# Earlier weight loads, five gathers at once and the last sums on three engines in a tower of convolution, attention and sorted experts

## Chip, cores and metric

One core of a Trainium2 chip. The time is that of the device in microseconds (us), one execution of the whole program; lower is better. Before the change it is 224.91 us, the median of 3 runs (224.11 to 225.05).

## What is computed

`x` is 8 batches of 375 rows of 128 numbers, all fp32. Three layers follow each other:

```python
# 1: per batch, on x transposed
h = silu(conv1d(xt, w_compress)); h = silu(conv1d(h, w_main, padding=1)); h = conv1d(h, w_expand)
y = layer_norm(h + x) * g + b
ff = gelu(y @ w_ff1.T + b_ff1) @ w_ff2.T + b_ff2
y = layer_norm(ff + y) * g2 + b2
h = max over 3 neighbouring rows of y            # 373 rows a batch
# 2: attention within a batch
n = layernorm(h); q = (n @ Wq + bq) * scale; k = n @ Wk + bk
h = h + softmax(q @ k.T) @ n
# 3: 8 experts, the best 2 for each row
n = layernorm(h); gates = softmax(relu(n @ gw1 + gb1) @ gw2 + gb2)
w, idx = top_k(gates, 2); w = softmax(w)
out = h + sum over the two: w * (gelu(n @ we1[e] + be1[e]) @ we2[e] + be2[e])
```

## The kernel before

Each of the five engines has its program written out as a string of pieces, `name.number`: `PE_ORDER` (TensorE, with the PSUM bank behind the colon), `DVE_ORDER` (VectorE), `ACT_ORDER` (ScalarE), `POOL_ORDER` (GpSimd) and `SP_ORDER` (the issuing queue of SyncE, SP here). Each engine goes through its string in order, and semaphores make a piece wait for its inputs. A piece that stands early in a string is thus issued early, and one that waits holds all that stand behind it. Rows of a batch lie as 125 partitions by 3 (`P`, `NJ`).

- Warm-up and first layer. `w.n` are `WARM[n]` plain 128x128 matmuls of the identity into a bank that is free (line 1000; each is two records in the trace). `a1` to `a7` are the convolutions, norms and transposes of the first layer (lines 1001 to 1084), `ft` and `fn` fold the two attention matrices into one (line 1038), `cb` and `bf` prepare bias columns. `xb` on GpSimd (line 528) adds a bias row to `x`, `p1` to `p4` on GpSimd (line 517) make 1/sqrt for the four norms, `l1` to `l4` apply them, on VectorE or ScalarE.
- Attention: `b1`, `bq`, `sc0` to `sc2`, `pt0` to `pt2`, `at` (lines 1091 to 1126), with `prob` and `prob_t` in SBUF.
- Experts. Batches 0, 6 and 7 (`DENSE`) go through all 8 experts: `D1` (line 1181, two per expert, 373 columns), `dg` (gelu on ScalarE, line 660; it reuses one of three `gd` tiles and so waits for `D2` of two experts before), `D2` (line 1188, 12 records), `da` (line 929, VectorE adds the weighted result to `x_sb`; each waits for the one before). They also fill TensorE's time between other pieces.
- Batches 1 to 5 (`SPARSE`) are sorted by expert. `scat` (line 541, GpSimd) scatters their rows into the DRAM buffer `xs`, a run of up to 2048 rows per expert. Then come 37 blocks of 128 rows (`NB` = 8 first blocks of each expert + 29 whose expert is known at run time alone). `rg.n` (line 422) loads a block's place from the table `tab_x` into a register of SP, `lx.n` (line 436) loads the block's rows into one of 18 `blk_x` tiles, `lw.n` (line 444) copies its expert's weights, 321 KB from `w_all`, into one of `WSLOTS` `blk_w` tiles. `lx.n` waits until `T.n-10` is done, `lw.n` until `yv` of the tile's last user is. Then `T.n` (transpose, line 1197), `xT.n` (copy), `L1.n` (line 1204), `gl.n` (gelu, ScalarE, line 671), `L2.n` (line 1213), `yv.n` (bias, VectorE, line 955, into one of `YBUF` tiles `yblk`), `so.n` (line 547: GpSimd scatters the block to its rows in `ys`).
- The end. `yl.n` (line 453) gathers both results of all rows of a sparse batch into `yg`, which has room for three batches, so `yl.3` and `yl.4` wait for the first sums. `fin.n` (lines 964 and 970) is six operations on VectorE that add them, times their weights in `w_top`, to `x_sb`. `out.n` and `od.n` (line 464) store the sparse and the dense batches, three DMAs each.

## Time and profile before

| | us |
|---|---|
| median of 3 runs | 224.91 |
| profiled execution, its time | 223.55 |
| its span, first to last instruction | 221.8 |
| TensorE busy | 206.9 (93%) |
| VectorE busy | 154.2 (70%) |
| ScalarE busy | 136.9 (62%) |
| GpSimd busy | 112.9 (51%) |

The engines are called PE (matmuls; PEld are its weight loads), DVE (VectorE), ACT (ScalarE), POOL (GpSimd) and SP. A `q` behind the name (SPq) marks the engine's sequencer, which issues DMAs. The page cuts the span into 40 slices of 5.5 us and gives each engine's busy share in tenths (9 stands for 90% or more). The chain is followed back from the last instruction to whatever released it. The granted clock of TensorE is 0.996 of full over the whole span.

### The profile page before, as it was taken

How to read it: one execution, taken by the hardware profiler on the slowest of the kernel's cores; microseconds unless marked ns; L12 is line 12 of the kernel's file. 1: busy time of each engine (PE TensorE's matmuls, PEld its weight loads, DVE VectorE, ACT ScalarE, POOL GpSimd, SP SyncE). 2: the span in 40 equal slices, each digit the busy share in tenths (PEclk: the TensorE clock that was granted, in tenths of full speed). 3: DMA queues.
4: the chain of work that ended last, by engine and by line, in shares of the span. 5: the costliest groups of instructions: out<-in, count | busy, mean ns of one | idle time of the engine just before them, and what ended most of it. 6: DMA issues, size and time to landing. Idle time of an engine off the chain costs nothing.

```text
span 221.8 us, 5472 instructions
## 1 busy us (share of the span) xinstructions
PE 206.9 (93%) x1575; PEld 169.1 (76%) x1575; DVE 154.2 (70%) x688; ACT 136.9 (62%) x302; POOL 112.9 (51%) x168
## 2 busy tenths in 40 slices
PE   6997897899999999999999999999999889899990
PEld 6875656668957986798778876889998778699780
DVE  6169899999898998887788953486435333234895
ACT  2124987998889688867578447646645456444430
POOL 7626676720740055747674776005777676572000
PEclk9999999999999999999999999999999999999998
DMA  5999999950010003111211121377696899822673
GB/s 128 247 269 298 318 405 405 401 197 3 0 35 1 3 0 83 50 35 49 70 47 36 38 69 60 74 235 248 192 311 201 296 295 303 286 90 74 189 221 105
DMA packets 25856, 35.30 MB, mean 159 GB/s; under 512 B 4067, under 2 KB 18566, under 8 KB 25827
## 3 DMA queue, kind: packets, MB, share of 16 engines
q1 hardware_dynamic: 23137, 30.79, 43.7%
q0 software_dynamic: 2240, 4.00, 5.8%
q8 instruction: 13, 0.21, 0.4%
q10 hardware_dynamic: 450, 0.16, 0.4%
q14 instruction: 16, 0.13, 0.2%
HBM read 10.61 MB, written 14.39 MB: 113 GB/s over the span
## 4 chain that ended last, share of the span: by engine, by line
PE 73%; DVE 8%; SPq 6%; ACT 5%; issue 4%; DMA 2%; POOL 1%; DVEq 0%; ACTq 0%
PE PS L1188 11%; PE PS L1181 10%; PE PS L1123 7%; PE PS L1105 7%; PE PS L1213 5%; PE PS L1204 5%; PE PS L1000 5%; PE PS L988 4%; PE PS L1112 4%; SPq L444 3%; PE PS L1100 3%; SPq L436 2%; PE PS L1017 2%; DVE acc L964 2%; DMA blk_x<-xs 2%
## 5 line engine op out<-in xcount | busy, mean ns | idle before, releaser
L547 POOL DMA_INDIRECT ys<-yblk,blk_x x37 | 36.0, 972 | 27.5 <-DVE yblk L955 19.3
L517 POOL TENSOR_TENSOR rstd<-mv,mhalf 125x3 f32<-125x3 f32 x32 | 27.7, 866 | 42.3 <-DVE mv L697 42.0
L541 POOL DMA_INDIRECT xs<-rows_x,pos_x x30 | 29.9, 998 | 13.3 <-issue 8.4
L660 ACT ACTIVATE gd<-PS,bias 128x373 f32<-128x373 f32 x48 | 27.1, 574 | 15.4 <-PE PS L1181 10.7
L1181 PE MATMUL PS<-xt_sb,w_all 128*128 128x373 f32 x96 | 35.7, 482 | 0.0
L1188 PEld LDWEIGHTS PS<-w_all,gd 128*125 128x125 f32 x288 | 33.6, 188 | 2.1
L1188 PE MATMUL PS<-w_all,gd 128*125 128x128 f32 x288 | 34.6, 273 | 0.0
L671 ACT ACTIVATE gb_t<-PS,blk_w 128x128 f32<-128x128 f32 x58 | 18.0, 365 | 14.2 <-issue 7.7
L929 DVE SCALAR_TENSOR_TENSOR x_sb<-PS,comb,x_sb 125x128 f32<-125x128 f32 x72 | 20.7, 342 | 5.8 <-PE PS L1188 4.9
L1181 PEld LDWEIGHTS PS<-xt_sb,w_all 128*128 128x128 f32 x96 | 15.7, 190 | 5.0 <-issue 0.9
L955 DVE TENSOR_TENSOR yblk<-PS,blk_w 128x128 f32<-128x128 f32 x29 | 8.4, 290 | 14.9 <-PE PS L1213 14.5
L1105 PE MATMUL PS<-xn_t,q_t 128*125 128x373 f32 x48 | 18.0, 488 | 0.0
L1123 PE MATMUL PS<-xn,prob_t 125*125 125x129 f32 (+1 forms) x144 | 17.6, 275 | 0.0
L1213 PE MATMUL PS<-blk_w,gb_t 128*128 128x128 f32 x116 | 17.4, 277 | 0.0
L1123 PEld LDWEIGHTS PS<-xn,prob_t 125*125 125x125 f32 (+1 forms) x144 | 16.7, 187 | 0.8 <-issue 0.4
L1204 PE MATMUL PS<-xb_t,blk_w 128*128 128x128 f32 x116 | 17.2, 275 | 0.0
L816 DVE COPY xb_t<-PS 128x128 f32<-128x128 f32 x27 | 7.8, 289 | 13.6 <-PE PS L1197 11.1
L1204 PEld LDWEIGHTS PS<-xb_t,blk_w 128*128 128x128 f32 x116 | 15.6, 191 | 1.8 <-issue 0.3
L1213 PEld LDWEIGHTS PS<-blk_w,gb_t 128*128 128x128 f32 x116 | 15.0, 191 | 0.7 <-issue 0.3
L830 DVE TENSOR_REDUCE nmax<-PS 125x1 f32<-125x373 f32 x24 | 12.8, 543 | 2.9 <-PE PS L1105 2.2
L636 ACT ACTIVATE prob_t<-PS 124x373 f32<-124x373 f32 (+1 forms) x23 | 9.9, 482 | 6.2 <-PE PS L1112 5.9
L630 ACT ACTIVATE prob<-PS,nmax 125x373 f32<-125x373 f32 x24 | 12.5, 574 | 1.4 <-DVE nmax L830 1.2
(201 smaller groups left out, 414.1 us busy)
## 6 DMA issues: line engine op xcount, KB each, us to landing
blk_w<-w_all SPq DMA_DIRECT2D x29, 321.0 KB, 3.0
xs<-blank SPq DMA_DIRECT2D x1, 8256.0 KB, 25.8
blk_x<-xs SPq DMA_DIRECT2D x37, 64.5 KB, 3.2
yg<-ys SPq DMA_DIRECT2D x5, 336.0 KB
xt_sb<-in_xt SPq DMA_DIRECT2D x4, 375.0 KB, 5.9
x_sb<-in_x SPq DMA_DIRECT2D x4, 336.0 KB
out<-x_sb SPq DMA_DIRECT2D x8, 168.0 KB
w_all<-in_we SPq DMA_DIRECT2D x1, 1024.0 KB
```

What stands on the lines that cost most here:

```text
L517: pool.tensor_tensor(rstd[i][:, n % 2, :], mv[i][:, n % 2, :, 1], mhalf[:], ALU.pow)\
L541: pool.indirect_dma_start(xs, bass.IndirectOffsetOnAxis(ap=pos_x[:, b // 2, s, i:i + 1], axis=0), rows_x[:, k, s, j, :], None, bounds_chec ...
L547: pool.indirect_dma_start(ys, bass.IndirectOffsetOnAxis(ap=blk_x[n % SLOTS][:, t, D:XW].bitcast(u32), axis=0), yblk[n % YBUF][:, t, :], No ...
L660: act.activation(gd[:, k % GD, c, 0:TP], of("D1", n)[:, 0:TP], ACT.Gelu, bias=bias128[:, 2 + k % E * HC + c:3 + k % E * HC + c]).then_inc( ...
L671: last = act.activation(gb_t[n % 2][:, c, :], of("L1", n)[:, c * BLK:(c + 1) * BLK], ACT.Gelu, bias=w[:, 2 * H + c:2 * H + c + 1])
L929: last = dve.scalar_tensor_tensor(flat(h2[:, b, :])[j], flat(of("D2", n)[0:P, :])[j], w[:, j, b % 2, e:e + 1], flat(h2[:, b, :])[j], ALU.m ...
L1105: pe.matmul(f[0:P, 0:TP], q_t[:, s, OFF[j]:OFF[j] + P], xn_t[:, s, :], start=True, stop=True)\
L1123: last = pe.matmul(f[0:P, j * (D + 1):(j + 1) * (D + 1)], prob_t[0:ROWS[c], s, c, OFF[j]:OFF[j] + P], xn3[0:ROWS[c], s, c, :], start=(c == ...
L1181: pe.matmul(f[:, 0:TP], w_all[:, k % E, c * 128:(c + 1) * 128], x32[:, DENSE[k // E], 0:TP], start=True, stop=True).then_inc(S["D1"], 1)
L1188: last = pe.matmul(f[0:P, j * D:(j + 1) * D], gd[:, n % GD, c, OFF[j]:OFF[j] + P], w_all[:, n % E, H + c * D:H + (c + 1) * D], start=(c == ...
L1204: last = pe.matmul(f[:, c * BLK:(c + 1) * BLK], w[:, c * 128:(c + 1) * 128], xb_t[n % 2][:], start=True, stop=True)
L1213: last = pe.matmul(f[:, t * D:(t + 1) * D], gb_t[n % 2][:, c, t * 128:(t + 1) * 128], w[:, H + c * D:H + (c + 1) * D], start=(c == 0), sto ...
```

## The change

- `WSLOTS` goes from 7 to 14 and `YBUF` from 6 to 12. The seven added weight tiles lie in a tile `late`, which `prob` and `prob_t` use before; `lw.15`, the first that goes there, waits for the last `at`. Eight of the `blk_x` tiles now lie in `blank`. The semaphores of the added tiles are reused ones.
- The gathers `yl` of the five sparse batches go into tiles of their own (two of them in `late`) and no longer wait for a sum.
- `fin.1` and `fin.3` leave VectorE: `fm.1` and `fm.3` on ScalarE multiply the gathered tile in place by the weights (six activations each), and GpSimd adds the two products with two `tensor_tensor` of 125x384.
- New orders on all engines, in which some copies change between VectorE and ScalarE, and `WARM` goes from (12, 15, 5, 3) to (22, 13, 4, 3, 1).

```diff
--- before.py
+++ after.py
@@ -52,9 +52,11 @@
 XW = D + 1
 SLOTS = 18
 LOADS = 10
-WSLOTS = 7
-YBUF = 6
+WSLOTS = 14
+OWN = 7
+YBUF = 12
 YG = 3
+assert NS <= YG + 3
 
 PER = ROWS_X // 128
 RI = max(k for k in range(1, 9) if PER % k == 0)
@@ the orders, their parts that the steps below follow
 PE_ORDER = """
-w.0:0 a1.0:5 w.1:0 ft.0:7 a2.0:6 a2.1:3 w.2:0 a3.0:1 a3.1:4 a1.1:3 cb.0:2 w.3:0 a2.2:7 a2.3:6 fn.0:0 a1.2:1 bf.0:4
+w.0:1 a1.0:0 w.1:2 a2.0:1 a2.1:4 ft.0:5 w.2:0 a3.0:2 a3.1:6 a1.1:5 cb.0:3 w.3:0 a2.2:5 a2.3:7 w.4:1 bf.0:0 fn.0:3
...
-g2.3:0 D1.21:1 D1.22:2 D1.23:0 D1.24:3 D1.25:1 D2.9:7 D2.10:6 D2.11:0 ct.1:2 ct.2:3 bd.1:1 T.0:5 D2.12:2 L1.0:5
+g2.3:6 D1.21:0 D1.22:7 D1.23:3 D1.24:1 D2.9:6 D1.25:4 D2.10:0 D2.11:2 T.0:3 ct.1:1 ct.2:7 L1.0:3 T.1:4 bd.1:1 L1.1:4
...
-L2.31:5 L1.32:1 T.34:2 D1.36:3 L1.33:0 L2.32:5 T.35:1 L1.34:2 L2.33:7 L1.35:6 T.36:0 L2.34:5 D1.37:1 L1.36:4 L2.35:6
-D1.38:2 L2.36:7 D2.15:0 D2.16:5 D1.39:3 D1.40:7 D2.17:1 D2.18:6 D2.19:7 D1.41:1 D1.42:6 D1.43:5 D1.44:2 D2.20:7
-D1.45:4 D1.46:3 D2.21:5 D1.47:1 D2.22:2 D2.23:0
+L1.30:4 T.32:3 L2.29:0 L1.31:2 D1.34:4 L2.30:3 T.33:2 L1.32:0 L2.31:3
+T.34:5 L1.33:6 L2.32:4 T.35:3 L1.34:5 L2.33:0 T.36:1 L1.35:3 L2.34:7 L1.36:4 D1.35:1 L2.35:7 D1.36:6 L2.36:5 D1.37:1
+D2.15:7 D1.38:4 D1.39:2 D2.16:6 D2.17:1 D2.18:0 D1.40:5 D1.41:6 D1.42:2 D1.43:5 D1.44:3 D2.19:7 D2.20:6 D1.45:5
+D2.21:0 D1.46:2 D1.47:7 D2.22:5 D2.23:2
 DVE_ORDER = """
-ft.0 a3.0 a3.1 l1.0 fn.0 cb.0 l1.1 bf.0 a3.2 a3.3 l1.2
+ft.0 a3.0 a3.1 cb.0 l1.0 bf.0 l1.1 a3.2 a3.3 l1.2 fn.0
...
-da.15 da.16 da.17 da.18 da.19 fin.0 fin.1 fin.2 da.20 da.21 fin.3 da.22 da.23 fin.4
+da.15 da.16 da.17 fin.0 da.18 da.19 da.20 fin.2 da.21 fin.4 da.22 da.23
 ACT_ORDER = """
...
-gl.34 gl.35 gl.36 dg.36 dg.37 dg.38 dg.39 dg.40 dg.41 dg.42 dg.43 dg.44 dg.45 dg.46 dg.47
+gl.36 dg.35 dg.36 dg.37 dg.38 dg.39 dg.40 dg.41 dg.42 dg.43 fm.1 fm.3 dg.44 dg.45 dg.46 dg.47
 POOL_ORDER = """
...
-so.27 so.28 so.29 so.30 so.31 so.32 so.33 so.34 so.35 so.36
+so.27 so.28 so.29 so.30 so.31 so.32 so.33 so.34 so.35 so.36 fin.1 fin.3
 SP_ORDER = """
-c4.1 c4.2 c4.3 c4.4 c4.5 rg.8 rg.9 rg.10 rg.11 rg.12 rg.13 rg.14 rg.15 od.0 rg.16 rg.17 rg.18 rg.19 rg.20 rg.21
-rg.22 rg.23 rg.24 rg.25 rg.26 lx.0 lx.1 lx.2 lx.3 lx.4 lx.5 lx.6 lx.7 lx.8 lw.8 lx.9 lw.9 lx.10 lw.10 lx.11 lw.11
...
-lx.27 lw.27 lx.28 lw.28 rg.35 lx.29 lw.29 lx.30 lw.30 lx.31 lw.31 lx.32 lw.32 lx.33 lw.33 lx.34 lw.34 rg.36 lx.35
-lw.35 lx.36 lw.36 yl.0 yl.1 yl.2 od.1 yl.3 out.0 yl.4 out.1 out.2 out.3 od.2 out.4
+c4.1 c4.2 c4.3 c4.4 rg.8 rg.9 rg.10 rg.11 rg.12 lw.8 rg.13 c4.5 lw.9 rg.14 lw.10 rg.15 lw.11 rg.16 lw.12 rg.17 lw.13
+rg.18 rg.19 rg.20 lw.14 lx.0 lx.1 lx.2 lw.15 lx.3 lw.16 lx.4 lx.5 lx.6 lx.7 od.0 lw.17 lx.8 lx.9 rg.21 lx.10 rg.22
...
+lx.22 lx.23 lx.24 lx.25 lx.26 lw.21 lw.22 lw.23 lx.27 rg.28 lw.24 lw.25 rg.29 lx.28 lx.29 rg.30 lw.26 lx.30 lw.27
+lw.28 rg.31 rg.32 lw.29 rg.33 lw.30 lx.31 lw.31 lx.32 lw.32 rg.34 rg.35 lx.33 lw.33 lw.34 lx.34 rg.36 lx.35 lx.36
+lw.35 lw.36 od.1 yl.0 yl.1 yl.2 yl.3 yl.4 out.0 out.1 out.2 out.3 out.4 od.2
@@ -146,7 +148,7 @@
 
 
 
-WARM = (12, 15, 5, 3)
+WARM = (22, 13, 4, 3, 1)
 
 
 ON_ACT = set(pieces(ACT_ORDER))
@@ -237,9 +239,10 @@
         xn_t = sb("xn_t", [D, 2, TP])
         q_t = sb("q_t", [D, 2, TE])
         nmax = sb("nmax", [P, 2, NJ])
-        prob = sb("prob", [P, 2, NJ, TP])
+        late = sb("late", [128, (WSLOTS - OWN) * WROW])
+        prob = late[0:P, 0:2 * NJ * TP].rearrange("p (s j t) -> p s j t", s=2, j=NJ)
         rinv = sb("rinv", [P, NJ])
-        prob_t = sb("prob_t", [P, 2, NJ, TE])
+        prob_t = late[0:P, 2 * NJ * TP:2 * NJ * (TP + TE)].rearrange("p (s j t) -> p s j t", s=2, j=NJ)
         h2 = x_sb
         xn4 = sb("xn4", [P, len(DENSE), NJ, D])
         rows_x = sb("rows_x", [128, NS, 2, NJ, XW])
@@ -276,16 +279,19 @@
         tab_e = sb("tab_e", [1, NDYN], i32)
         tab_x = sb("tab_x", [1, NDYN], i32)
 
-        blk_x = [sb(f"blk_x{i}", [128, NT, XW]) for i in range(SLOTS)]
-        blk_w = [sb(f"blk_w{i}", [128, WROW]) for i in range(WSLOTS)]
+        blank = sb("blank", [128, RI, XW])
+        blk_x = [sb(f"blk_x{i}", [128, NT, XW])[:] for i in range(SLOTS - RI)] + [blank[:, r:r + 1, :] for r in range(RI)]
+        blk_w = [sb(f"blk_w{i}", [128, WROW])[:] for i in range(OWN)]\
+            + [late[:, i * WROW:(i + 1) * WROW] for i in range(WSLOTS - OWN)]
         xb_t = [sb(f"xb_t{i}", [D, BLK]) for i in range(2)]
         gb_t = [sb(f"gb_t{i}", [128, HC, BLK]) for i in range(2)]
         yblk = [sb(f"yblk{i}", [128, NT, D]) for i in range(YBUF)]
-        yg = sb("yg", [P, YG, 2, NJ * D])
+        yg_own = sb("yg", [P, YG, 2, NJ * D])
+        yg = [yg_own[:, i, :, :] for i in range(YG)]\
+            + [late[0:P, i * 2 * NJ * D:(i + 1) * 2 * NJ * D].rearrange("p (s d) -> p s d", s=2) for i in range(NS - YG)]
         acc = sb("acc", [P, NJ, D])
 
         tiny = sb("tiny", [1, 1])
-        blank = sb("blank", [128, RI, XW])
 
         gd = sb("gd", [128, GD, HC, TE])
         comb = sb("comb", [P, len(DPAIRS), NI, E])
@@ -324,11 +330,15 @@
         s_blank = sem("s_blank_out")
         s_copy = [sem(f"s_copy{i}") for i in range(2)]
         s_scat = sem("s_scat")
-        s_yl = [sem(f"s_yl{i}") for i in range(YG)]
+        s_yl = [(sem(f"s_yl{i}"), 0) for i in range(YG)]
         s_out = sem("s_out")
         s_bx = [sem(f"s_bx{i}") for i in range(LOADS)]
-        s_bw = [sem(f"s_bw{i}") for i in range(WSLOTS)]
         s_so = [sem(f"s_so{i}") for i in range(YBUF)]
+
+
+        s_yl += [(S["wt"], 16 * 9), (S["rows"], 16), (s_blank, 16)]
+        s_bw = ([(s, 32) for s in s_x] + [(s, 16) for s in s_xt] + [
+            (S[v], 16 * m) for v, m in (("wc", 1), ("we", 2), ("b64", 2), ("wm", 2), ("rows6", 1), ("wmid", 3))])[:WSLOTS]
 
         def wait(eng, name, value):
             if value > 0:
@@ -361,8 +384,9 @@
             if n < E:
                 eng.wait_ge(S["be1"], 1)
                 return w_all[:, n, :]
-            eng.wait_ge(s_bw[(n - E) % WSLOTS], 16 * ((n - E) // WSLOTS + 1))
-            return blk_w[(n - E) % WSLOTS][:]
+            s, first = s_bw[(n - E) % WSLOTS]
+            eng.wait_ge(s, first + 16 * ((n - E) // WSLOTS + 1))
+            return blk_w[(n - E) % WSLOTS]
 
         def xn4_of(n):
 
@@ -433,29 +457,29 @@
                         sp.wait_ge(s_scat, 16 * NI * NS)
                     wait(sp, "T", n - LOADS + 1)
                     wait_so(sp, n - SLOTS)
-                    sp.dma_start(blk_x[i][:], xs[bass.ds(row_of_block[n], BLK), :].rearrange("(p t) d -> p t d", t=NT))\
+                    sp.dma_start(blk_x[i], xs[bass.ds(row_of_block[n], BLK), :].rearrange("(p t) d -> p t d", t=NT))\
                         .then_inc(s_bx[n % LOADS], 16)
                 if name == "lw":
                     k = n - E
                     if k == 0:
                         sp.wait_ge(S["be1"], 1)
+                    if k == OWN:
+                        wait(sp, "at", B)
                     if k >= WSLOTS:
                         wait(sp, "yv", n + 1 - WSLOTS)
-                    sp.dma_start(blk_w[k % WSLOTS][:], w_all[:, bass.ds(row_of_block[n] // CAP, 1), :].rearrange("p o d -> p (o d)"))\
-                        .then_inc(s_bw[k % WSLOTS], 16)
+                    sp.dma_start(blk_w[k % WSLOTS], w_all[:, bass.ds(row_of_block[n] // CAP, 1), :].rearrange("p o d -> p (o d)"))\
+                        .then_inc(s_bw[k % WSLOTS][0], 16)
                 if name == "yl":
                     if n == 0:
                         for m in range(NB - YBUF, NB):
                             wait_so(sp, m)
-                    if n >= YG:
-                        wait(sp, "ob", n - YG + 1)
                     for lo, hi in SPLIT:
-                        sp.dma_start(yg[lo:hi, n % YG, :, :],
+                        sp.dma_start(yg[n][lo:hi, :, :],
                                      ys[2 * T * n:2 * T * (n + 1), :]
-                                     .rearrange("(s p j) d -> p s (j d)", s=2, j=NJ)[lo:hi]).then_inc(s_yl[n % YG], 16)
+                                     .rearrange("(s p j) d -> p s (j d)", s=2, j=NJ)[lo:hi]).then_inc(s_yl[n][0], 16)
                 if name in ("out", "od"):
                     if name == "out":
-                        wait(sp, "ob", n + 1)
+                        wait(sp, *summed(n))
                         b = SPARSE[n]
                     else:
                         wait(sp, "da", E * (n + 1))
@@ -541,6 +565,13 @@
                     pool.indirect_dma_start(xs, bass.IndirectOffsetOnAxis(ap=pos_x[:, b // 2, s, i:i + 1], axis=0),
                                             rows_x[:, k, s, j, :], None, bounds_check=ROWS_X - 1, oob_is_err=False)\
                         .then_inc(s_scat, 16)
+                if name == "fin":
+
+                    k, b = RANK_POOL["fin", n], SPARSE[n]
+                    wait(pool, "fm", RANK_ACT["fm", n])
+                    pool.tensor_tensor(h2[:, b, :], h2[:, b, :], yg[n][:, 0, :], ALU.add).then_inc(S["obp"], 1)
+                    wait(pool, "obp", 2 * k - 1)
+                    pool.tensor_tensor(h2[:, b, :], h2[:, b, :], yg[n][:, 1, :], ALU.add).then_inc(S["obp"], 1)
                 if name == "so":
                     wait(pool, "yv", n + 1)
                     for t in range(NT):
@@ -609,6 +640,15 @@
                     wait(act, "ht", n // 2 - 1)
                     act.activation(y2_t[:, n // 2 % 2, n % 2, :], of("a7", n)[:, 0:T], ACT.Identity, bias=cols[:, 5:6],
                                    scale=cols[:, 4:5]).then_inc(S[nth("y2", n)[0]], 1)
+                if name == "fm":
+
+                    gathered(act, n)
+                    w = shares(n)
+                    for s in range(2):
+                        for j in range(NJ):
+                            last = act.activation(flat(yg[n][:, s, :])[j], flat(yg[n][:, s, :])[j], ACT.Copy,
+                                                  scale=w[:, s, j, :])
+                    last.then_inc(S["fm"], 1)
                 if name == "hv":
                     wait(act, "hr", n + 1)
                     wait(act, "h2", NJ * (n - 1))
@@ -956,19 +996,17 @@
                                       w.unsqueeze(1).broadcast_to([128, NT, D]), ALU.add)\
                         .then_inc(S["yv"], 1)
                 if name == "fin":
-                    dve.wait_ge(s_yl[n % YG], 32 * (n // YG + 1))
-                    wait(dve, "ob", n)
-                    b = SPARSE[n]
-                    w = w_top[:, b // 2, :, :].rearrange("p s (j b) -> p s j b", b=2)
+                    gathered(dve, n)
+                    k, b, w = RANK_DVE["fin", n] - 1, SPARSE[n], shares(n)
+                    wait(dve, "ob", k)
                     for j in range(NJ):
-                        last = dve.scalar_tensor_tensor(acc[:, j, :], flat(yg[:, n % YG, 0, :])[j], w[:, 0, j, b % 2:b % 2 + 1],
-                                                        flat(h2[:, b, :])[j], ALU.mult, ALU.add)
-                        last.then_inc(S["acc"], 1)
+                        dve.scalar_tensor_tensor(acc[:, j, :], flat(yg[n][:, 0, :])[j], w[:, 0, j, :],
+                                                 flat(h2[:, b, :])[j], ALU.mult, ALU.add).then_inc(S["acc"], 1)
                     for j in range(NJ):
                         if j != 1:
-                            wait(dve, "acc", NJ * n + (2, 2, 3)[j])
-                        last = dve.scalar_tensor_tensor(flat(h2[:, b, :])[j], flat(yg[:, n % YG, 1, :])[j],
-                                                        w[:, 1, j, b % 2:b % 2 + 1], acc[:, j, :], ALU.mult, ALU.add)
+                            wait(dve, "acc", NJ * k + (2, 2, 3)[j])
+                        last = dve.scalar_tensor_tensor(flat(h2[:, b, :])[j], flat(yg[n][:, 1, :])[j], w[:, 1, j, :],
+                                                        acc[:, j, :], ALU.mult, ALU.add)
                     last.then_inc(S["ob"], 1)
 
         @block.tensor
```

## Rows read from the trace of the kernel before

**Rows 1.** Page, part 1 and 2: busy time, then tenths in 40 slices of 5.5 us.

```profile
PE 206.9 (93%) x1575; PEld 169.1 (76%) x1575; DVE 154.2 (70%) x688; ACT 136.9 (62%) x302; POOL 112.9 (51%) x168
...
PE   6997897899999999999999999999999889899990
```

**Rows 2.** Timeline of the start: start us, us, engine, line, operation, tiles, count.

```profile
2.04 4.28 PE L1000 MATMUL PS<-ident 128*128 128x128 f32 x24 [2.04 <-DVE comb_t L711]
...
7.03 3.62 PE L1000 MATMUL PS<-ident 128*128 128x128 f32 x30
...
7.21 0.57 ACT L576 ACTIVATE hc<-PS,bias 128x375 f32<-128x375 f32 x1 [2.39 <-PE PS L1006]
...
10.48 0.27 PE L1038 MATMUL PS<-ident,wk_sb 128*128 128x128 f32 x1
...
10.79 1.21 PE L1017 MATMUL PS<-hc,wm_d 64*64 64x192 f32 x24
```

**Rows 3.** Landing of the loads of xt_sb and of wm_d (answers by tile).

```profile
DMA to landing us min/median/max: 3.3/5.9/6.7
...
DMA to landing us min/median/max: 3.7/4.6/5.4
```

**Rows 4.** Waits of TensorE and of SP: us in total, times, longest.

```profile
PE PS L1197 <- DMA blk_x<-xs: 2.6, 3, 1.0
...
SPq L444 <- DVE yblk L955: 1.4, 1, 1.4
```

**Rows 5.** Chain that ended last, sparse stage and end: start us, us, what.

```profile
186.66 4.08 DMA blk_x<-xs
...
192.02 0.45 PE PS L1204 x4
...
192.57 0.63 PE PS L1181 x2
...
198.72 2.63 PE PS L1188 x24
```

**Rows 6.** Timeline of SP's queue: start us, us of issue, line, tiles.

```profile
139.29 5.35 SPq L436 DMA_DIRECT2D blk_x<-xs  x9
...
173.61 0.49 SPq L444 DMA_DIRECT2D blk_w<-w_all  x1
...
175.80 0.50 SPq L444 DMA_DIRECT2D blk_w<-w_all  x1
...
186.66 0.38 SPq L436 DMA_DIRECT2D blk_x<-xs  x1
...
187.98 0.77 SPq L436 DMA_DIRECT2D blk_x<-xs  x1
```

**Rows 7.** Timeline of the end.

```profile
202.53 2.56 SPq L453 DMA_DIRECT2D yg<-ys  x6
...
207.37 0.87 DVE L964 SCALAR_TENSOR_TENSOR acc<-yg,w_top,x_sb 125x128 f32<-125x128 f32 x3
...
213.40 2.79 PE L1188 MATMUL PS<-w_all,gd 128*125 128x128 f32 x24
...
218.39 0.87 DVE L970 SCALAR_TENSOR_TENSOR x_sb<-yg,w_top,acc 125x128 f32<-125x128 f32 x3
```

**Rows 8.** Timeline around 18 us and 27 us.

```profile
17.99 2.90 POOL L528 TENSOR_TENSOR x_sb<-x_sb,row_be 125x384 f32<-125x384 f32 x3
...
18.06 2.91 DVE L703 TENSOR_SCALAR n<-r,mv,rstd 125x128 f32<-125x128 f32 x3
...
27.40 1.25 ACT L565 ACTIVATE n<-r,nmr,rstd 125x128 f32<-125x128 f32 x3
```

**Rows 9.** Answers by source line, 422 (registers) and 436 (gathers).

```profile
L422 SPq TENSOR_LOAD <-tab_x x29: 261/273/665, 122.4 to 189.5; - x29
...
DMA to landing us min/median/max: 2.2/3.2/3.9
```

**Rows 10.** Timeline, the transpose of the last block (T.36).

```profile
195.41 0.27 PE L1197 MATMUL PS<-ident,blk_x 128*128 128x128 f32 x1
```

More of the change, by code:

```diff
@@ new lines @@
+a2.7:5 a7.0:6 a5.1:7 a3.6:1 a3.7:0 a4.4:6 a7.1:2 a6.2:7 a6.3:5 a4.5:3 hr.0:4 a5.2:1 hr.1:6 a6.4:1 a7.2:7 a4.6:6
+b1.0:2 a7.3:5 b1.1:3 bq.0:2 a6.5:7 sc0.0:4 sc1.0:6 bq.1:2 sc2.0:3 a7.4:5 sc0.1:1 sc1.1:2 a4.7:6 pt0.0:3 pt1.0:0
+pt2.0:4 sc2.1:6 a5.3:4 at.0:0 pt0.1:1 pt1.1:3 pt2.1:5 hr.2:2 a6.6:6 at.1:4 hr.3:5 a7.5:2 h1.0:1 a6.7:3 D1.0:0 b1.2:7
+D1.1:5 D1.2:1 h1.1:6 bq.2:7 a7.6:5 g1.0:0 b1.3:6 sc0.2:2 sc1.2:7 bq.3:1 g2.0:6 a7.7:4 sc2.2:0 sc0.3:1 sc1.3:5 hr.4:2
+pt0.2:3 pt1.2:0 D2.0:7 pt2.2:0 sc2.3:1 hr.5:3 at.2:4 pt0.3:0 pt1.3:6 pt2.3:1 rk.0:5 D1.3:0 at.3:1 ct.0:2 D2.1:5
@@ L163, in ranks @@
     return rank
[L166 removed]
+RANK_ACT, RANK_DVE, RANK_POOL = ranks(ACT_ORDER), ranks(DVE_ORDER), ranks(POOL_ORDER)
 BANK = {tuple(word.split(":")[0].split(".")): int(word.split(":")[1]) for word in PE_ORDER.split()}
@@ L345, in wait_nth, with summed, gathered, shares @@
                 wait(eng, *nth(name, n))
+        def summed(n):
+            return ("obp", 2 * RANK_POOL["fin", n]) if ("fin", n) in RANK_POOL else ("ob", RANK_DVE["fin", n])
+        def gathered(eng, n):
+            s, loads = s_yl[n]
+            eng.wait_ge(s, loads + 32)
+        def shares(n):
+            return w_top[:, SPARSE[n] // 2, :, :].rearrange("p s (j b) -> p s j b", b=2)[:, :, :, SPARSE[n] % 2:SPARSE[n] % 2 + 1]
         def normed_by(i, n):
```

83 lines of the change are left out of this document (38 added, 45 removed).

## The prediction

> **What bounds the kernel now.** I read the page first [rows 1]: TensorE is busy 93% of the span and 9 tenths or more of nearly every slice between 42 and 200 us. The time is therefore TensorE's work plus the stretches in which it starves or does filler, plus what follows its last matmul. The change leaves the matmuls as they are (only warm-up ones are added), so I looked for these stretches in three places.
>
> The start: its timeline [rows 2] shows w.0 (24 records, two per matmul) until 6.3 us, the first convolution a1.0 at once behind it, w.1 (30 records in 3.62 us, 0.12 each) until about 10.4, then a2.0 at 10.79. The landing views [rows 3] say that this wasn't needed: the first load of `xt_sb` was issued at 1.28 and landed 3.3 us later, at 4.6; the second of `wm_d`, issued at 2.65, took 5.4 and was in at 8.1; ScalarE's part of a1.0 ended at 7.8. So a1.0 and a2.0 stood behind warm-up, not behind data.
>
> The sparse stage, 143 to 199 us: here TensorE waited 2.6 us for gathered rows of `xs` [rows 4], and the chain runs through such a gather from 186.7 to 190.7 [rows 5], with SP's queue ahead of it. SP's timeline [rows 6] shows why: SP issues without a rest. A pair of a gather (lx, 0.38) and a weight load (lw, 0.50) comes every 1.33 us with the address arithmetic; a pair with a register load (rg) takes 2.1 to 2.2, so an rg costs about 0.8 between DMAs.
>
> The end: the last matmul (D2.23) ends at 216.2, but VectorE has been busy without a gap since 206.6 with the five sums `fin` (1.6 each) between the `da` of the dense batches; it does da.22 and da.23 until 217.7, fin.4 until 219.26, then SP issues three stores, and the span ends at 221.8, 2.5 behind the last sum [rows 7].
>
> **Change part by part.** All against this execution: span 221.8, 223.55 with what lies around it, which is 1.4 below the median of 224.91.
>
> *Warm-up.* w.0 goes from 12 to 22 matmuls, w.1 from 15 to 13, w.2 from 5 to 4, a w.4 of one is added, and ft (two transposes, 0.3 between 10.48 and a2.0) goes behind a2.1. 20 records more ahead of a1.0 are 20 x 0.12 = 2.4 us. At a2.0: +2.4, -4 x 0.12 = -0.5, -0.3: +1.6. Behind that the shift stays, for a3.0 needs ScalarE's hc2, then VectorE's r1 and the norm, and GpSimd's three additions `xb` (17.99 to 20.9), which hold VectorE's l1.1 [rows 8], come after the norm's p1.1 in both orders. From 42 us on TensorE is full [rows 1], so nothing absorbs it. Bounds: 0 (the idle time of TensorE between 17 and 44 us, 7 to 9 tenths busy by the same row, takes it up) to 2.4. I take +1.6, since the dependencies between are unchanged and no load lands late.
>
> *Weight tiles 7 to 14, orders of SP.* The table is ready at 122.4 [rows 9], the scatters at 139.3 [rows 6]. Before, SP did 19 rg (0.55 each when in a row) and the store od.0 in between and waited 3.5 us for od.0's data. Now it does 13 rg, seven lw (lw.8 to lw.14, 0.66 each) and c4.5: 7.2 + 4.6 + 0.9 = 12.7 us, inside the same 17. So these seven loads cost nothing there. Behind lx.0, SP has 7 lw less (-4.6 us), but 6 rg more (6 x 0.8 = +4.8) and od.0 (+1.1); what it saves is the wait for a free weight tile (1.4 [rows 4]). Its last issues come only about 1 us earlier than 192.3. What TensorE asks for: adding up its work along PE_ORDER from the end of D2.11 at 142.0 (T 0.11, L1 and L2 0.45, D1 0.63, D2 1.31, from [rows 5]), T.36 would be due at 189.7 and ran at 195.4 [rows 10]: 5.7 late, of which about 1.7 had gathered before T.21 and 4 after, behind gathers. In the new orders the gathers lx.18 to lx.30 come 1 to 6 us ahead of before, so the stalls of 174 and 182 go. But lx.31 stands behind three rg and three lw: by SP's prices it is issued at about 181.6 and lands 3.2 later [rows 9], at 184.8, while T.31 is due at 180.4 + 1.7 = 182.1: 2.7 late; T.34 and T.35 add 0.4 each in the same way. 3.5 in place of about 4.2: -0.7. Bounds: -3.5 (SP keeps ahead everywhere) to +2.4 (the rival below).
>
> *12 result tiles.* VectorE waited once, 0.3, for one. Nothing: GpSimd needs 1.28 us for a scatter and is nearly full from 150 to 201, so deeper tiles only lengthen its queue. so.36 follows yv.36 by 1.3 us as before.
>
> *The end.* Count from the end of L2.36 (198.6 before; call it T). Behind it TensorE has D1.37 to D1.47 and nine D2, 11 x 0.63 + 9 x 1.31 = 18.7 us (17.5 before, the 1.3 more stood ahead of T: no change in sum). yl.0 is issued at about T + 4.1, as at 202.5 before, behind od.1; the five gathers now go out together, 0.8 each, and a load of 375 KB follows another by some 1.6 us, an estimate from fin.0's start 4.8 after yl.0's issue [rows 7]: yl.1 lands by T + 9.4, yl.3 by T + 12.6. ScalarE's fm.1 and fm.3 are 12 activations of 125x128 from SBUF, one every 0.4 (three in 1.25 [rows 8]): 4.8 us, between dg.43 (ends T + 10.3) and dg.44. So dg.44 starts at T + 15.1, dg.45 ends at 16.35, and D2.22, due at 16.1, starts at 16.45: +0.35 on TensorE. GpSimd's two additions of 125x384 (1.0 each [rows 8]) end at T + 15 and T + 17.3, ahead of need. VectorE is left with three `fin`, the last (fin.4) between da.21 and da.22, until T + 17.9; da.22 ends at 18.8 and da.23 1.1 after D2.23. Before it was 3.1 from D2.23's end to that of the last sum (216.2 to 219.26): -2.0. od.2 has the same three issues as out.4 had.
>
> *The port.* GpSimd's three additions of 17.99 to 20.9 made three multiply-subtracts of VectorE take 1.0 us each in place of 0.34 [rows 8]. The sums may meet fin.1 and fin.3 on GpSimd; no row here has such a pair long enough to tell, so the cost is between nothing and one such hold, 0.7, on fin.4, whose end has about 0.5 of slack before da.23 can start. I take +0.1 and keep 0 to +0.7; nothing speaks for a gain.
>
> The Trainium skill (GPSIMD Engine Reference, section 8) states that GpSimd shares its SBUF interfaces with VectorE, with contention for instructions "in a 2-port perf mode or with two SBUF inputs". By that the sums, with two SBUF inputs, would be held and the sum be at the upper end, which is part of the third rival.
>
> *Sum.* 221.8 + 1.6 - 0.7 + 0.35 - 2.0 + 0.1 = 221.1, that is 0.7 less. Against the median: 224.2.
>
> **Rivals.**
> - The warm-up is absorbed, or SP keeps ahead: for it speaks that orders and tiles fit each other and that gathers 18 to 30 come earlier; against, that TensorE is full from 42 on. The first alone gives 221.1 - 1.6 = 219.5, the second alone 221.1 - 2.8 = 218.3: 222.6 and 221.4 by the median; both, 219.8.
> - Slower: SP's queue costs more than I charge. The place is the stretch from rg.27 to lx.31, the price 0.9 to 1.0 for each of the 16 rg behind lx.0 (one cost up to 0.9 in [rows 6]) and 3.9 to landing, the longest seen [rows 9]. T.31 then is 5.5 late in place of 2.7, and the sum is 221.1 + 2.9 = 224.0, 227 by the median. It decides from where lx.31 is issued later than 183 (in this execution's time), with the warm-up's 1.6 not taken up.
> - The end goes wrong: a tail in which ScalarE's 12 activations take 0.48 each and the port holds VectorE: D2.22 1.3 late and the last sum 0.6 late, 1.3 more than my sum: 222.4, or 225.5 by the median.
> - The extra tiles change nothing at all (SP is the bound either way) and only start and end count: 221.8 + 1.6 + 0.35 - 1.9 = 221.9, 225.0 by the median.
>
> **How the numbers follow.** A measurement of this kernel can tell about 0.5%, 1.1 us. My forecast (0.7 faster, from 1.7 faster to 0.3 slower) has 0.35; absorbed or ahead 0.25; slower through SP 0.18; a bad end 0.10; nothing from the tiles 0.12. Faster by over 0.5%: all of the second and a third of the first, 0.37. Slower by over 0.5%: the SP rival and part of the bad end, 0.23. The rest, 0.40, is within. For 8 in 10 the range must take in the middle of the absorbed case (222.0) and most of the SP rival (226.6). The forecast's own range is 223.2 to 225.2.
>
> **What would show it.** In the changed profile a1.0 should start near 8.6 us and a2.0 near 12.4; a saturated TensorE from 43.5; lx.0 near 141; waits for `blk_x` gathered in one stall around T.31 and none at 174 to 182; dg.44 about 5 us behind dg.43 and a TensorE gap of 0.3 ahead of D2.22; VectorE's last operation a da, 1.1 behind the last matmul, and span's end 2.5 behind it. Wrong would be: a1.0 at 8.6 but TensorE full at 42 all the same, stalls behind gathers over 4 us in sum, or a last sum on any engine behind da.23.

## The result, and the profile after

The changed kernel takes 227.01 us (median of 17 runs, 224.25 to 228.74) where the kernel before takes 224.93 beside it: ratio 1.0086, 95% interval 1.0057 to 1.0115, some 2 us slower. Four of the 17 are slow runs, over 1.5% above the fastest; the ratio is of the others, whose median is 226.74, and prices below are counted from that. Forecast were 224.2 and a range up to 226.6. The profiled execution of the kernel after took 228.74 us, 1.7 above its median, with a span of 227.0; that of before (span 221.8) was 1.4 below its median. So the traces stand 5.2 us apart, the medians 2.1, and I use the traces for places and the medians for prices.

The code has moved by some 40 lines. In the rows of after T is L1235, L1 is L1242, L2 is L1251, D1 is L1219, D2 is L1226 and `dg` L700; `da` is L969, `fin` on VectorE L1003 and L1008, `fm` on ScalarE L649, GpSimd's additions L572 and L574; the gathers `lx` are L460, the weight loads `lw` L470, warm-up is L1038.

The page of after: busy time, then tenths in 40 slices, here of 5.7 us, for TensorE and for the clock granted to it.

```profile
PE 212.7 (94%) x1591; PEld 174.3 (77%) x1591; DVE 153.1 (67%) x681; ACT 138.0 (61%) x309; POOL 117.2 (52%) x168
...
PE   6999798899999999999999999999999967999982
...
PEclk9999999999999999999999999999999995899998
```

PE is 5.8 us busier than in [rows 1] though the matmuls are the same but for 16 records of warm-up; where the clock is low each matmul takes longer (below). The 33rd and 34th slice (182 to 193 us) hold a 6 and a 7, and the clock has a 5 and an 8 in the 34th and 35th (187 to 199 us). Before had no such place.

The start, timeline of TensorE, to be held against [rows 2]:

```profile
2.04 7.47 PE L1038 MATMUL PS<-ident 128*128 128x128 f32 x44 [2.04 <-DVE comb_t L751]
9.45 0.85 PE L1044 MATMUL PS<-xt_sb,wc_p 128*64 128x375 f32 x4
...
13.33 1.21 PE L1055 MATMUL PS<-hc,wm_d 64*64 64x192 f32 x24
```

a1.0 comes at 9.45, 3.2 later than before, and a2.0 at 13.33, 2.5 later. The granted clock rose from 1.2 to 2.4 GHz at 6.92 us here and at 4.89 in before, both times during the warm-up.

TensorE's waits (in total, times, longest), and the stretch around T.31, timeline and windows (length, then busy time of PE, PEld, DVE, ACT and POOL, granted clock, DMA share, GB/s):

```profile
PE PS L1235 <- DMA blank<-xs: 3.3, 1, 3.3
...
PE PS L1226 <- ACT gd L700: 0.6, 1, 0.6
```

```profile
184.59 0.79 PE L1219 MATMUL PS<-xt_sb,w_all 128*128 128x373 f32 x2
...
184.92 0.37 SPq L460 DMA_DIRECT2D blank<-xs  x1
...
188.65 0.47 PE L1235 MATMUL PS<-ident,blank 128*128 128x128 f32 x1 [3.27 <-DMA blank<-xs]
188.92 1.06 PE L1251 MATMUL PS<-blk_w,gb_t 128*128 128x128 f32 x4
...
191.48 1.45 PE L1219 MATMUL PS<-xt_sb,w_all 128*128 128x373 f32 x2
```

```profile
170.00:180.00 10.00, 10.00 (x81) 9.10 (x80) 4.50 (x18) 5.28 (x16) 7.56 (x9) 1.00 0.74 250
180.00:190.00 10.00, 6.64 (x47) 5.68 (x46) 2.24 (x8) 3.76 (x12) 5.22 (x6) 0.89 0.80 271
190.00:200.00 10.00, 10.00 (x62) 9.11 (x62) 2.87 (x11) 5.59 (x17) 4.87 (x6) 0.77 0.54 184
```

The three waits of [rows 4], 2.6 us in all, have become one, of 3.3 us, at the place that the prediction named: lx.31 is issued at 184.92, T.31 runs at 188.65. What it didn't name stands right behind: two D1 matmuls take 0.79 us ahead of the stall and 1.45 at 191.48, four L2 0.61 at full clock (195.73 to 196.34) and 1.06 here. The clock was at 1.2 GHz from 187.8, still within the wait, to 194.7.

The end, to be held against [rows 7]:

```profile
213.78 1.86 ACT L649 ACTIVATE yg<-yg,w_top 125x128 f32<-125x128 f32 x6 [0.40 <-DMA yg<-ys]
...
216.84 1.63 DVE L1003 SCALAR_TENSOR_TENSOR acc<-yg,w_top,x_sb 125x128 f32<-125x128 f32 x3
216.95 1.86 ACT L649 ACTIVATE late<-late,w_top 125x128 f32<-125x128 f32 x6 [1.31 <-DMA late<-ys]
...
218.40 1.63 DVE L1008 SCALAR_TENSOR_TENSOR x_sb<-yg,w_top,acc 125x128 f32<-125x128 f32 x3
...
218.72 1.93 ACT L700 ACTIVATE gd<-PS,bias 128x373 f32<-128x373 f32 x4
218.89 0.99 POOL L572 TENSOR_TENSOR x_sb<-x_sb,late 125x384 f32<-125x384 f32 x1 [1.09 <-ACT late L649]
...
219.87 2.86 PE L1226 MATMUL PS<-w_all,gd 128*125 128x128 f32 x24 [0.65 <-ACT gd L700]
219.95 0.85 DVE L969 SCALAR_TENSOR_TENSOR x_sb<-PS,comb,x_sb 125x128 f32<-125x128 f32 x3
219.96 1.00 POOL L574 TENSOR_TENSOR x_sb<-x_sb,late 125x384 f32<-125x384 f32 x1
...
222.35 1.86 DVE L969 SCALAR_TENSOR_TENSOR x_sb<-PS,comb,x_sb 125x128 f32<-125x128 f32 x6
```

fm.3 waits 1.31 for its gather, so dg.44 comes at 218.72 and D2.22 0.65 late. The last matmul ends at 222.73, VectorE 1.5 behind it (3.1 before), and the span 2.8 behind that.

To see where the lag arises I laid the matmuls of both traces beside each other by the work done. TensorE is some 2.5 to 3.0 us later than before from 50 to 145 us, 2.4 at 165, 1.1 at 181 (the first two stalls of before are gone), 5.3 at 191, 5.7 at 208; the last matmul ends 6.5 later, the span 5.2.

### The profile page after: what moved, and what is told of

Same layout as the page of the kernel before. It is cut to its first block, busy times and chain, and to the rows that moved or that the text cites. A ratio compares the mean times of both kernels' runs of the same rounds, so it can differ in the third digit from the quotient of the medians.

```text
span 227.0 us, 5502 instructions
## 1 busy us (share of the span) xinstructions
PE 212.7 (94%) x1591; PEld 174.3 (77%) x1591; DVE 153.1 (67%) x681; ACT 138.0 (61%) x309; POOL 117.2 (52%) x168
## 4 chain that ended last, share of the span: by engine, by line
PE 68%; DVE 16%; SPq 6%; issue 4%; DMA 2%; ACT 2%; POOL 0%; DVEq 0%; ACTq 0%
PE PS L1219 12%; PE PS L1226 11%; PE PS L1161 6%; PE PS L1143 6%; PE PS L1251 5%; PE PS L1242 5%; PE PS L1038 5%; PE PS L1150 3%; SPq L470 3%; PE PS L1026 3%; DVE stat L732 3%; DVE n L743 3%; PE PS L1138 2%; SPq L446 2%; DVE x_sb L969 2%
## 5 line engine op out<-in xcount | busy, mean ns | idle before, releaser
L1219 PE MATMUL PS<-xt_sb,w_all 128*128 128x373 f32 x96 | 36.2, 488 | 0.0
L1226 PEld LDWEIGHTS PS<-w_all,gd 128*125 128x125 f32 x288 | 33.6, 187 | 3.2 <-ACT gd L700 1.2
L700 ACT ACTIVATE gd<-PS,bias 128x373 f32<-128x373 f32 x48 | 26.3, 573 | 15.1 <-PE PS L1219 10.2
L1226 PE MATMUL PS<-w_all,gd 128*125 128x128 f32 x288 | 34.7, 272 | 0.6 <-ACT gd L700 0.6
L578 POOL DMA_INDIRECT ys<-yblk,blk_x x21 | 20.4, 973 | 23.5 <-DVE yblk L995 18.8
L969 DVE SCALAR_TENSOR_TENSOR x_sb<-PS,comb,x_sb 125x128 f32<-125x128 f32 x72 | 20.7, 343 | 6.0 <-PE PS L1226 5.2
L1219 PEld LDWEIGHTS PS<-xt_sb,w_all 128*128 128x128 f32 x96 | 16.2, 193 | 5.3 <-issue 0.7
L578 POOL DMA_INDIRECT ys<-yblk,blank x16 | 15.6, 973 | 7.4 <-DVE yblk L995 4.1
L1161 PEld LDWEIGHTS PS<-xn,late 125*125 125x125 f32 (+1 forms) x144 | 16.6, 187 | 1.8 <-issue 1.7
L1161 PE MATMUL PS<-xn,late 125*125 125x129 f32 (+1 forms) x144 | 17.7, 276 | 0.0
L711 ACT ACTIVATE gb_t<-PS,late 128x128 f32<-128x128 f32 x28 | 8.8, 366 | 10.6 <-PE PS L1242 5.6
L1038 PE MATMUL PS<-ident 128*128 128x128 f32 x86 | 13.1, 318 | 2.0 <-DVE comb_t L751 2.0
L670 ACT ACTIVATE late<-PS,nmax 125x373 f32<-125x373 f32 x24 | 13.0, 570 | 3.0 <-DVE nmax L870 2.6
L1038 PEld LDWEIGHTS PS<-ident 128*128 128x128 f32 x86 | 12.3, 229 | 2.9 <-POOL ident L499 2.0
L676 ACT ACTIVATE late<-PS 124x373 f32<-124x373 f32 (+1 forms) x23 | 10.2, 482 | 6.1 <-PE PS L1150 5.9
L711 ACT ACTIVATE gb_t<-PS,blk_w 128x128 f32<-128x128 f32 x30 | 9.4, 365 | 7.1 <-issue 4.6
```

The source lines that it names most:

```text
L578: pool.indirect_dma_start(ys, bass.IndirectOffsetOnAxis(ap=blk_x[n % SLOTS][:, t, D:XW].bitcast(u32), axis=0), yblk[n % YBUF][:, t, :], No ...
L670: act.activation(prob[:, n % 2, j, :], of(name, n)[0:P, 0:TP], ACT.Exp, bias=nmax[:, n % 2, j:j + 1]).then_inc(S["prob"], 1)
L700: act.activation(gd[:, k % GD, c, 0:TP], of("D1", n)[:, 0:TP], ACT.Gelu, bias=bias128[:, 2 + k % E * HC + c:3 + k % E * HC + c]).then_inc( ...
L711: last = act.activation(gb_t[n % 2][:, c, :], of("L1", n)[:, c * BLK:(c + 1) * BLK], ACT.Gelu, bias=w[:, 2 * H + c:2 * H + c + 1])
L969: last = dve.scalar_tensor_tensor(flat(h2[:, b, :])[j], flat(of("D2", n)[0:P, :])[j], w[:, j, b % 2, e:e + 1], flat(h2[:, b, :])[j], ALU.m ...
L1038: pe.matmul(f[:, 0:D], ident[:], ident[:], start=True, stop=True)
```

## Experiments

Medians, and in brackets the ratio to the kernel before with its 95% interval; the kernel before ran beside each, with a median of 224.5 to 224.9. Most kernels have six runs. Where two changed kernels ran at different times, the difference of their ratios is given or their intervals are named.

**The single causes, on the kernel after.** e1, shorter warm-up:

```diff
-WARM = (22, 13, 4, 3, 1)
+WARM = (12, 13, 4, 3, 1)
```

> The kernel after, with 12 warm-up matmuls in w.0 in place of 22 (WARM 12, 13, 4, 3, 1), nothing else. In the two traces TensorE stands 2.5 to 2.8 us later from 20 us on to 130 us, more than the 1.6 that the prediction took. Theory (the shift is the 20 added records, 0.12 each at the full clock, and nothing behind them takes it up): a1.0 starts near 7 us in place of 9.5, the whole curve comes 2.3 to 2.5 earlier, 224.6 by the median in place of 227.0. Rival (the start is set by when the granted clock rises, 4.9 us in the trace of before and 6.9 in that of after, and the kernel waits for data behind a short warm-up): a1.0 comes earlier, but at 30 us the shift is back, gain under 0.7, 226.5.

222.34 (ratio to before 0.9888, 0.9851 to 0.9925), 4.4 less than after, nearly twice what was forecast. The theory holds for the start: 1.9 earlier from 37 to 138 us, although the clock rose later still (7.71). But more than that came from something else: the waits for gathers are 2.1 in two places, ahead of T.34 and of T.0,

```profile
PE PS L1235 <- DMA blank<-xs: 1.5, 1, 1.5
...
PE PS L1235 <- DMA blk_x<-xs: 0.6, 1, 0.6
```

and the clock stays full. lx.31 came 4.7 earlier (180.26); 3.6 of this lx.0 has already, which stood 2.9 behind the last scatter in place of 4.7. Warm-up isn't separable from the stall here; e7 takes it alone.

e2, gathers earlier in SP's queue:

```diff
-rg.18 rg.19 rg.20 lw.14 lx.0 ... lx.7 od.0 lw.17 lx.8 lx.9 rg.21 lx.10 rg.22
+rg.18 rg.19 rg.20 lw.14 rg.21 rg.22 lx.0 ... lx.7 lw.17 lx.8 lx.9 lx.10
-lw.28 rg.31 rg.32 lw.29 rg.33 lw.30 lx.31 lw.31
+lw.28 rg.31 lx.31 rg.32 lw.29 rg.33 lw.30 lw.31
-lw.35 lw.36 od.1
+lw.35 lw.36 od.0 od.1
```

> The kernel after, with another order of SP's queue only: rg.21 and rg.22 go ahead of lx.0, where the queue stood still for 1.7 us, od.0 goes to the end of the queue's loads, and lx.31 goes right behind rg.31, ahead of rg.32, lw.29, rg.33 and lw.30. In the trace of after T.31 waits 3.4 us for its gather, issued at 184.9 and landed 3.7 later, and the granted clock then falls to half for 6.8 us. Theory: the gather is issued by 181, the stall is under 1 us, the clock doesn't fall: 2.5 us less from the stall and up to 2.9 from the clock, 222.5 to 224.5. Rival (SP is the bound whatever the order, a stall only moves to the weight loads lw.27 to lw.29 or to T.33): TensorE waits as long elsewhere between 180 and 196, 226 to 227.5.

223.27 (0.9909, 0.9875 to 0.9943), 3.5 less than after by an order alone. lx.31 went out at 179.0, T.31 ran at 184.8, no wait for a gather is left, and the clock is full in both windows:

```profile
180.00:190.00 10.00, 10.00 (x79) 9.03 (x79) 3.90 (x15) 6.61 (x21) 7.56 (x9) 1.00 0.78 266
190.00:200.00 10.00, 8.91 (x64) 7.58 (x64) 2.23 (x9) 4.43 (x14) 7.01 (x8) 1.00 0.46 143
```

e3, filler in the stall, which parts the stall from the clock:

```diff
-D1.32:7 T.31:2
+D1.32:7 w.5:2 T.31:2
-WARM = (22, 13, 4, 3, 1)
+WARM = (22, 13, 4, 3, 1, 14)
```

> The kernel after, with 14 more warm-up matmuls of the identity (28 records, 3.1 to 3.3 us at the full clock) right ahead of T.31, whose gather is late anyway by 3.4 us. The result isn't touched. Theory (the fall of the granted clock to half is a consequence of TensorE's stall, and costs 2.9 us by the shift between the two traces): T.31 starts when it did, the clock stays at 2.4 GHz, and the time falls by up to 2.9, to 224.5 to 226. Rival (the clock falls for another reason, or the fall costs nothing): the same time, 227, or 3 us more where the gather wasn't late in a usual run.

225.93 (1.0039, 1.0008 to 1.0069): 0.8 less than after, 1.1 by the ratios, with 28 records more. The two intervals just touch. The stall is still there, only filled:

```profile
185.12 0.79 PE L1219 MATMUL PS<-xt_sb,w_all 128*128 128x373 f32 x2
185.75 3.29 PE L1038 MATMUL PS<-ident 128*128 128x128 f32 x28
189.18 0.33 PE L1235 MATMUL PS<-ident,blank 128*128 128x128 f32 x1
...
190.69 0.48 PE L1219 MATMUL PS<-xt_sb,w_all 128*128 128x373 f32 x1
```

T.31 isn't earlier, but the work behind it keeps its speed, and in the trace the lag to after goes from +0.65 ahead of the stall to -1.96 behind it: 2.6 us is what the fallen clock cost there. By the medians it is 0.8 to 1.1, for it seems not to fall in every run: the mean granted clock is 0.981 to 0.989 in ten of the 17 runs of after, and never below 0.994 in the twelve of e3. Of the 13 runs of after that are counted, the seven below 0.99 have a mean time of 226.7, the six others of 226.1. The theory holds; its size is about 1 us, not 2.9.

**Part by part from the kernel before.** e7, long warm-up alone:

```diff
-WARM = (12, 15, 5, 3)
+WARM = (22, 15, 5, 3)
```

> The kernel before with w.0 of 22 matmuls in place of 12, nothing else. Theory (20 records more ahead of a1.0 cost 2.4 us and nothing takes them up): 227.2 by the median, TensorE's curve 2.4 later from a1.0 to the end. Rival (part is taken up between 17 and 44 us, where TensorE was 7 to 9 tenths busy): 225.5 to 226.5. Rival (the gathers come earlier relative to TensorE, since SP keeps its own pace, and the stalls of 2.6 us go): about 225.

226.80 (1.0092, 1.0057 to 1.0127): 2.0 more. In its trace a1.0 is at 8.58 and TensorE 2.36 later from 45 to 170 us, constant to 0.01; nothing takes it up. Behind the sparse stage it is 3.2, for the waits for gathers are 3.0 in place of 2.6.

e4, the code of after with all orders and the warm-up of before:

> The code of the kernel after (14 weight tiles, 12 result tiles, five gather tiles that wait for no sum) with all orders and the warm-up of the kernel before: tiles alone. The five gathers go out without waiting, VectorE still does all five sums. The prediction held that only the wait of 1.4 us of SP for a weight tile goes. Theory: SP's queue runs 1.4 ahead from 170 us on, the stalls for gathers fall from 2.9 to about 1.5, the end is as before (VectorE's five sums behind each other): 223.5. Rival (SP is as late as before, its prices alone count): 224.9. Rival (deeper tiles let GpSimd's scatters pile up, and the gathers at the end come later): 225.5 or more.

223.06 (0.9927, 0.9894 to 0.9959): 1.8 less. In the trace TensorE is 1.0 ahead of before at 175; SP's wait for a weight tile is gone. TensorE's waits are 0.8 ahead of T.28 and 1.3 ahead of one L1, 2.1 in place of 2.6. A little more than theory gave, on the same side; the code of the change is a gain.

e5, the end of the change on top of e4 (fm.1 and fm.3 between dg.43 and dg.44, fin.1 and fin.3 on GpSimd, SP's od.1 ahead of the five gathers and all stores behind them); of its edit VectorE's order:

```diff
-da.15 da.16 da.17 da.18 da.19 fin.0 fin.1 fin.2 da.20 da.21 fin.3 da.22 da.23 fin.4
+da.15 da.16 da.17 da.18 da.19 fin.0 da.20 fin.2 da.21 fin.4 da.22 da.23
```

> The kernel of e4 (code of after, orders and warm-up of before) with one thing more, the end as in the change: fin.1 and fin.3 as fm on ScalarE between dg.43 and dg.44 and two additions each on GpSimd, VectorE with fin.0, fin.2 and fin.4 (the last between da.21 and da.22), od.1 ahead of the five gathers, all stores behind them. e4 was 223.06 by the median. Theory (the prediction's terms for the end: 2.0 less behind the last matmul, 0.35 more ahead of D2.22, 0.1 for the port; the trace of after shows 1.3 less and 0.8 more): between 1.6 and 0.5 less than e4, 221.5 to 222.5. Rival (the twelve activations delay dg.44 and with it D2.22 by as much as the end saves): the same as e4, 223.1, or more.

223.88 (0.9957, 0.9924 to 0.999), 0.8 more than e4 where I expected 0.5 to 1.6 less. The intervals of e4 and e5 overlap, so that it costs is not shown; that the saving didn't come is. The timeline of the end says why:

```profile
209.99 0.99 POOL L572 TENSOR_TENSOR x_sb<-x_sb,yg 125x384 f32<-125x384 f32 x1 [9.57 <-ACT yg L649]
210.31 2.97 DVE L1003 SCALAR_TENSOR_TENSOR acc<-yg,w_top,x_sb 125x128 f32<-125x128 f32 x3
...
211.06 0.99 POOL L574 TENSOR_TENSOR x_sb<-x_sb,yg 125x384 f32<-125x384 f32 x1
212.14 1.00 POOL L572 TENSOR_TENSOR x_sb<-x_sb,late 125x384 f32<-125x384 f32 x1
213.03 2.89 PE L1226 MATMUL PS<-w_all,gd 128*125 128x128 f32 x24 [0.34 <-ACT gd L700]
213.21 1.68 DVE L1008 SCALAR_TENSOR_TENSOR x_sb<-yg,w_top,acc 125x128 f32<-125x128 f32 x3
```

fin.2 takes 4.6 us in place of 1.6 while GpSimd's four additions run, and the last da ends 3.1 behind the last matmul, as the last sum did before.

e10 cuts these additions to one column of 384, leaving most of the sums of two batches out:

```diff
-pool.tensor_tensor(h2[:, b, :], h2[:, b, :], yg[n][:, 0, :], ALU.add)
+pool.tensor_tensor(h2[:, b, 0:1], h2[:, b, 0:1], yg[n][:, 0, 0:1], ALU.add)
```

> The kernel of e5 with GpSimd's four additions cut from 384 columns to one, so that most of the sums of two batches is left out. In the trace of e5 four operations of fin.2 on VectorE took 0.82, 1.15, 1.16 and 1.15 us in place of 0.34 while these additions ran, and the last sum ended 3.1 behind the last matmul, as far as before. Theory (the additions hold VectorE's operations with two SBUF inputs, and this is what ate the saving of the end): fin.2 takes 1.6 in all, VectorE ends 1.5 behind the last matmul, 1 to 1.6 less than e5's 223.88, 222.3 to 222.9. Rival (the gathers' landing or ScalarE sets the pace of VectorE's tail): the same as e5, 223.9.

221.51 (0.9867, 0.9822 to 0.9913), 2.4 less than e5, 2.0 by the ratios, more than forecast. All of VectorE's operations are short again (0.87 for three), and it ends 0.9 behind the last matmul:

```profile
211.43 0.18 POOL L572 TENSOR_TENSOR x_sb<-x_sb,yg 125x1 f32<-125x1 f32 x1 [9.60 <-ACT yg L649]
...
211.75 0.87 DVE L1003 SCALAR_TENSOR_TENSOR acc<-yg,w_top,x_sb 125x128 f32<-125x128 f32 x3
```

The span of this trace, 221.3, is only 0.3 under that of e5. The rest went in the sparse stage: TensorE waited 2.15 ahead of one L1, and behind it two D1 take 1.15 in place of 0.79, with the clock at 1.2 GHz from 189.3 to 192.7:

```profile
188.06 0.68 PE L1242 MATMUL PS<-xb_t,late 128*128 128x128 f32 x4 [2.15 <-issue]
...
189.03 1.15 PE L1219 MATMUL PS<-xt_sb,w_all 128*128 128x373 f32 x2
```

In e5 the same place had a wait of 1.7 and the clock stayed full.

**Towards a better kernel.** e6 joins e1 and e2:

> Both edits of e1 (w.0 with 12 matmuls) and e2 (rg.21 and rg.22 ahead of lx.0, od.0 late, lx.31 right behind rg.31) on the kernel after. e1 alone gave 222.34, e2 alone 223.27. In e1 TensorE waited 2.1 us for gathers, in e2 none. Theory (warm-up and late gather are two causes, and e1 got its second half by letting SP's queue run further ahead of TensorE): from e2 the warm-up's 2.4 go, from e1 the last stalls, 1.5 to 2.1: 220.5 to 221. Rival (with TensorE 2 us earlier the gathers are late again, as all of SP's queue hangs on the scatters): 222 to 222.5, no better than e1.

221.72 (0.9881, 0.9828 to 0.9935), 0.6 under e1 by the medians but the same by the ratios (0.9888): theory isn't met, and the rival is nearer, with 1.8 us of waits for gathers back, ahead of T.0 and T.34. e8 takes w.0 down to 6 matmuls:

> The kernel of e6 with w.0 of 6 matmuls in place of 12. The load of xt_sb landed at 4.6 us in the trace of before, and a1.0 ran at 6.3 there and at 7.4 in e1. Theory (warm-up ahead of a1.0 is pure delay): a1.0 near 5.3 to 6, 0.7 to 1.4 less than e6. Rival (the granted clock rises only after this work, at 4.9 to 8.2 us in the traces so far; what runs at 1.2 GHz in its place is a1.0 and w.1, and a2.0 waits for the second load of wm_d, in at 8.1, and for ScalarE's part of a1.0): within 0.5 of e6.

220.34 (0.9808, 0.9763 to 0.9854), 1.4 less than e6, run beside it: even there, warm-up ahead of a1.0 is delay. a1.0 ran at 4.87, its first part at the low clock, which rose at 6.23. e9 is e8 with all five sums on VectorE, and without fm and GpSimd's additions; of its edit VectorE's order:

```diff
-da.15 da.16 da.17 fin.0 da.18 da.19 da.20 fin.2 da.21 fin.4 da.22 da.23
+da.15 da.16 da.17 fin.0 da.18 da.19 da.20 fin.1 fin.2 da.21 fin.3 fin.4 da.22 da.23
```

> The kernel of e8 with the part of the change undone that moves two sums: fin.1 and fin.3 are back on VectorE (da.20 fin.1 fin.2 da.21 fin.3 fin.4 da.22 da.23), no fm on ScalarE, no addition on GpSimd. e5 against e4 said that the moved sums cost 0.5 to 0.8 in the orders of before. Theory (the moved sums cost what they save, through ScalarE ahead of dg.44 and through VectorE's held operations): e9 is e8 within 0.5, 219.9 to 220.9, the gap ahead of D2.22 is gone and VectorE ends 2.5 to 3 behind the last matmul in place of 1.5. Rival (in the orders of after the moved sums are the gain of 1.6 at the end that the trace shows): 221.5 to 222.

221.85 (0.9836 to 0.9914 around 0.9875), 1.5 more than e8. My theory falls, the rival holds: in the orders of after the moved sums are worth 1.5, though the ends of the two intervals overlap. There fin.0 goes ahead of da.18, VectorE has slack, and the 1.0 us that it is held for in e8 is absorbed: it ends 1.6 behind the last matmul in e8, 4.3 in e9.

e11 puts each late gather right behind its register load, or one weight load further (... rg.31 lx.31 rg.32 lx.32 lw.29 rg.33 lw.30 lx.33 lw.31 lw.32 rg.34 lx.34 lw.33 rg.35 lx.35 lw.34 rg.36 lx.36 lw.35 lw.36):

> The kernel of e8, its SP queue changed once more: lx.32, lx.33, lx.34 and lx.35 each right behind the register load that they need, the weight loads lw.29 to lw.34 behind them. In the trace of e8 TensorE waited 0.9 ahead of T.33 and 0.7 to 0.9 ahead of T.34, 1.6 in all. Theory: these waits go, 1 to 1.6 less than e8's 220.34, 218.8 to 219.4. Rival (SP is simply full: the weight loads are now late by what the gathers are early, and L1 waits in place of T): 220.3.

219.53 (0.9787, 0.9744 to 0.983), 0.8 less than e8, 0.5 by the ratios, and not clear of the noise; in its trace no wait for a gather is left. e12 also has w.1 of 6 matmuls in place of 13, WARM = (6, 6, 4, 3, 1):

> The kernel of e11 with w.1 of 6 matmuls in place of 13. In the trace of e8 a1.0 ran at 4.9 and a2.0 at 9.4; ScalarE's part of a1.0 ends about 1.1 behind it, and the second load of wm_d was in at 8.1 in the trace of before. Theory (w.1 is delay too): a2.0 at 8.6 to 8.8, 0.6 to 0.8 less than e11. Rival (a3 waits for ScalarE's and VectorE's parts, which hang on the loads of x and the weights, or the granted clock rises later by as much): within 0.4 of e11.

218.19 (0.9719, 0.9685 to 0.9753), 1.3 less than e11 beside it, more than the 0.6 to 0.8 forecast, and the fastest: 2.8% under the kernel before with tiles, end and matmuls of the change. Its TensorE waits for no gather; a wait of 1.1 ahead of one L1 is left.

**Does the late scatter come from the weight loads?** In after lx.0 stood 4.7 behind the last scatter, in before 2.5. e13 moves lw.12 to lw.14 from ahead of lx.0 to behind lx.2:

> The kernel after with lw.12, lw.13 and lw.14 moved from ahead of lx.0 to behind lx.2 in SP's queue, nothing else. In the trace of after the last scatter is issued at 138.2 and lx.0, which waits for it, at 142.9, 4.7 later, with 0.66 and 0.53 of the DMA engines busy; before it was 2.5 (136.8 and 139.3) at 0.16 and 0.31. Theory (the weight loads put into SP's wait slow the scatters' landing, and the gathers' whole queue starts 2 us later for it): lx.0 by 141, but lx.3 on no earlier than in after, for the three loads stand there now; the stall at T.31 stays within 1 of 3.4 and the time is 226 to 227. Rival (the late landing has nothing to do with the loads): lx.0 still 4.4 or more behind the last scatter, the queue 1.6 later in all, 227.5 to 228.5.

228.33 (1.017, 1.0122 to 1.0217). The scatter goes out at 137.66, lx.0 at 141.89, still 4.2 behind, though the DMA share between is 0.10, in after 0.53 (windows of after, then of e13):

```profile
138.00:142.00 4.00, 4.00 (x22) 2.89 (x21) 1.77 (x22) 3.56 (x5) 0.98 (x1) 1.00 0.53 186
```

```profile
138.00:142.00 4.00, 4.00 (x26) 3.16 (x25) 2.10 (x25) 3.94 (x7) 0.63 (x1) 1.00 0.10 28
```

The theory (lx.0 by 141) falls and the rival holds, but for 0.2 at lx.0: the loads were free where the change put them, and moved behind lx.0 they cost 1.6 us. TensorE now waits 1.1 for gathers ahead of T.8 and T.11 and the same 3.3 ahead of T.31. Why the landing differs stays open. e14 does the same on e12, with rg.23 and rg.24 ahead of lx.0:

> The kernel of e12 with the same three loads behind lx.2, and rg.23 and rg.24 ahead of lx.0 in their place. In the trace of e12 the last scatter was issued at 132.8 and landed at 135.5, 2.7 later, while SP itself was busy until lx.0 at 137.15: SP was late there, not the scatter. Theory: lx.0 goes to 135.6 to 136.2, but TensorE waited for no gather in e12 and asks for T.0 at 139.1 anyway, so nothing is gained: 218.2 within 0.4. Rival (T.0 and the stage behind it come earlier with lx.0): 217 or less.

218.62 (0.9783, 0.9728 to 0.9839), e12 within the noise: lx.0 stood 2.9 behind the last scatter in place of 4.3 (in e12 SP itself was busy until then), and nothing came of it, for TensorE waits for no gather in either.

## Why the prediction was wrong, point by point

- *Warm-up, +1.6.* Right in kind: fully paid, nothing absorbed. e7 gives 2.0 by the median, for four records more. At a2.0 it is 2.5 between the traces, since the clock rose 2.0 later in after than in before, and 2.0 us at half speed are 1.0 us of work. By e8 and e12 even shorter warm-up was faster.
- *Weight tiles and SP's orders, -0.7.* This is the step that failed, and in two ways. First its sum. It set 3.5 us of stalls against "about 4.2" before, but [rows 4] has 2.6 for before, in three waits, and the trace no other wait of TensorE between 144 and 199 us; the rest of the 4.2 was work that the adding up of single prices had left short. After had 3.3, so the forecast for after was nearly right, all of it ahead of T.31 (2.7 forecast) and none ahead of T.34 and T.35, and the term was +0.7, not -0.7. It is the largest mis-sized term. e3, where the clock stays full, bears it out: TensorE loses some 0.8 to before between 165 and 208 us.
- Second what it didn't contain: it added waits as if only their sum counted. Before had three of 0.8 to 1.0 us with the clock full throughout; after had one of 3.3, and the clock fell in it, which cost 0.8 to 1.1 us by the medians (e3) and 2.6 in the trace. The Trainium skill (TensorE: Matmul & The Clock Gate, HAM oscillation — how this bites in real kernels) says that matmuls which wait long for data start cold at half rate when it comes; the trace agrees (0.77 of full from 190 to 200 us). I hadn't weighed it. As e2 shows, the stall and its wake together cost 3.5, from an order that a few moves mend. The code alone gained 1.8 (e4) and the warm-up cost 2.0 (e7), so by the 1.8 of the whole change the new orders and the end together cost some 1.6, an estimate from these medians.
- *Where the stall came from.* From lx.0 to lx.31 SP took 42.0 us where 42.3 had been priced. But lx.0 was issued at 142.9 where 141 was forecast, 4.7 behind the last scatter in place of 2.5. Nothing in the prediction had that, and its cause stays open (e13). The prices for the whole queue behind lx.0 (-4.6, +4.8, +1.1, -1.4) also make 0.1 earlier and not "about 1"; the last weight load came at 195.5, 0.7 later than before when the 2.5 of the start are taken off.
- *End, 0.35 - 2.0.* D2.22 was 0.65 late, since I had fm.3's gather land ahead of fm.3, and it came 1.31 behind. From the last matmul to the span's end it is 4.3 in place of 5.6: -1.4 where -2.0 was forecast, as VectorE ends 1.5 behind it and not 1.1, and the stores 2.8 behind that and not 2.5. In sum -0.7 in place of -1.65. Nor is the saving a property of the edit: none in the orders of before (e5, +0.8, within the noise of zero), 1.5 in those of after (e9).
- *Port, +0.1, bound 0.7.* In after VectorE was held 1.5 us in fin.2 (two of its operations take 1.10 us in place of 0.34), but on slack; in e5 2.9, and on the path, where the bound of 0.7 was far too low: with the additions cut e5 is 2.0 to 2.4 faster (e10). What I read as "one such hold" comes once for each addition that meets a sum. The operations da, with one input in PSUM, took 0.85 for three beside the same additions (219.95), no more than elsewhere. The Trainium skill (SBUF — State Buffer, Who interferes with whom) says that a VectorE instruction with two SBUF inputs contends with a GpSimd one that reads SBUF; that is what the rows show.
- *Rivals.* The time is that of "SP's queue costs more" (227), but not by its mechanism: the stall was 0.6 longer than forecast, not 2.8, the price of the queue was right, and lx.31, at 184.92, is at 182.4 when the 2.5 of the start are taken off, ahead of the 183 that was its sign. That the times agree is chance. "The tiles change nothing" is refuted by e4. None of the three signs of being wrong came: they looked neither at the clock nor at what before had waited.

In the traces the account closes. TensorE's last matmul ends 6.5 later: 2.5 from the start, 0.7 from the stalls, 2.6 from the clock, 0.65 ahead of D2.22. What follows it is 1.4 shorter, and the span 5.2 longer, 5.8 more than forecast: 0.9 from warm-up, 1.4 from the stalls, 2.6 from the clock, 0.9 from the end. By the medians all is smaller: 2.0 from warm-up, 0.8 to 1.1 from the clock, and with 0.7 and -0.7 for stalls and end from the one trace this makes 2.8 to 3.1 where 1.8 is measured. The trace of after is a long one of its kind; which term is smaller in a usual run stays open.

## What to carry to other kernels

List the waits of the bounding engine one by one, not their sum: if one of them grows past all that the trace of before holds, price the work behind it at the low clock too. Take the waits of the kernel before from its trace, not from a sum of single prices that is short of the measured time. A deeper buffer is worth what the issuing queue lets through, so look which load goes out last before its due time (e2: 3.5 us by the queue's order alone). Work that moved from VectorE to GpSimd cost VectorE some 0.7 us again here for each GpSimd addition that met one of its sums, so give VectorE slack there first.

## What the hardware showed that I had not expected

- TensorE's clock rose at 4.9, 5.0, 5.0, 5.1, 5.3, 5.5, 6.9, 7.0, 7.6, 7.7 and 8.2 us in eleven traces (before, e5, e10, e7, e4, e13, after, e6, e2, e1, e3) whose warm-up begins at 2.04 with the same 24 records. Half of the 3.3 us between first and last, 1.6, is my estimate of what two traces can differ by in their first 10 us with no cause that their instructions show.
- One idle stretch of 3.3 us late in the kernel took the clock to 1.2 GHz for 6.8 us. In e13 a stall of the same 3.3 had it down for 3.4, and in e10 one of 2.15 as well; in e5 one of 1.7 didn't, nor in e1 two of 0.6 and 1.5 far apart.
- Where SP waited for the scatters, lx.0 stood 4.2 to 4.7 us behind the last one's issue in after, e3 and e13, and 2.3 to 2.7 in before, e4, e5, e7 and e10; in e1 and e14, where SP didn't wait, they had landed by 2.9. In the others SP came later itself. Weight loads aren't the cause (e13); nothing here shows what is.
